# Local attention in blocks of 32 queries with 160 keys, one relative mask, and one DMA round trip for q and k

## The chip, the cores and the metric

The kernel runs on one core of one Trainium2 chip, as one program in fp32. The metric is device time in microseconds (us) of that core, the median of several runs. TensorE (PE in the rows, PEld for its weight loads), VectorE (DVE), ScalarE (ACT) and GpSimd (POOL) compute; SyncE (SP) issues the DMAs of the stage that is changed. The two "streams" below are the two batches.

## The reference, cut to what matters

A first part (a recurrent attention layer) is not touched. The second part has two layers; in each, after the projection of q, k and v (8 heads of 64), q and k are normalised and rotated, and every query sees the keys of its own window of 128 and of the window before, as far as they are at most 128 positions back:

```python
bk, bv = (look_around(bk), look_around(bv))        # the window before, and the own one
sim = jnp.einsum('bhwid,bhwjd->bhwij', bq, bk)     # bq is q * 8
i = bt[:, :, None]
j = btk[:, None, :]
mask = (i < j) | (i > j + WINDOW) | (j == -1)      # WINDOW = 128
sim = jnp.where(mask, -jnp.finfo(sim.dtype).max, sim)
attn = jax.nn.softmax(sim, axis=-1)
out = jnp.einsum('bhwij,bhwjd->bhwid', attn, bv)
```

Then follow the output projection, a layer norm, and a gated MLP (hidden size 682). There are 2 batches of 4096 positions, so 32 windows for each batch and layer.

## The kernel before

The program has five stages: `setup`, `mix`, `scan`, `gate`, and `local`, which holds both layers of the second part and takes the span from about 2257 us to its end. Only `local` is changed.

`local_stage` steps through 64 units (u = 0 to 63: 32 windows of layer 0, then 32 of layer 1) for each of two streams s. A **half-step** `half(s, u, w, l)` does the attention of stream s, unit u (w = u % 2 is the slot of its keys), and beside it the end of the attention and the MLP of the other stream o (unit `um`), and projects stream s's next unit. There are 128 half-steps. Each engine runs its own list of work per half-step, and each list is written out by hand, in a `half` for each engine; semaphores tie them. No engine overtakes in its own list.

TensorE's list is: `values` of o for head pairs 0 and 1; `scores` of s for pairs 0 and 1; (layer 1: `turn_out`); `values` 2 and 3; `scores` 2 and 3; `project_out`; `project` k, `mean`, `project` v, `variance`, `project` q; `hidden`; `out`. `scores(2)` and `scores(3)` wait until `row_max` has emptied the PSUM banks of two pairs before.

q and k come out of VectorE's 32x32 block transposes (`turn_q`, `turn_k`) and need the blocks moved between partition quarters. This is done by a DMA round trip through DRAM: SP writes `q1` to `qz` and reads it back in four DMAs into `qT` (`write_q`, `read_q`), and so with k (`kz`, `kT`, at a later place of the list). The probabilities go the same way: `turn_p` turns one pair of heads into `pb`, `write_p` writes a group g of two pairs, `read_p` reads it back in four DMAs into `pT`; `values` waits for them. SP's list is: `read_q`; a store; loads of the next window; `write_p` 0; `write_k`; `write_p` 1; `read_p` 0; `read_k`; `read_p` 1; `write_q`. A read waits first until the write has landed.

For the scores of one head, 64 rows of `qT` are the weights (64x128) and 256 keys (two slots of 128) stream past them. The two heads of a pair lie in the two row halves of the array. `row_max` adds the mask and takes the maximum, `exponent` (ScalarE) and `normalise` (GpSimd) work on 256 keys a head. Since the slot of a window's own keys alternates, there is a mask for each slot order, and `remask` rewrites a half of one.

## Time and profile before

| | us |
|---|---|
| median of 3 runs | 4971.94 |
| lowest, highest | 4968.18, 4976.64 |
| the profiled execution | 4966.22 |
| span of the profiled execution | 4964.4 |
| `local` stage, from its first GpSimd instruction to the end | 2256.95 to 4964.4 |

The profile page gives busy time by engine over the span; since the five stages differ, the stretches of the local stage are read apart. A timeline lists instructions of one engine in order of time, merged where one follows another of the same kind; an fp32 matmul stands in it as two records, each with its weight load on PEld. In SP's timeline the time is that in which SP is held by issuing, not that of the transfer.

### The profile page before, as it was taken

The numbers are of one execution on the slowest core, as the hardware profiler recorded it, in microseconds if no ns is written. First come the engines' busy times: TensorE is split into PE (matmuls) and PEld (weight loads), VectorE is DVE, ScalarE is ACT, GpSimd is POOL, SyncE is SP. The second block draws the span as 40 slices with busy tenths as digits, with TensorE's granted clock in tenths as the row PEclk, the third lists the DMA queues.
The fourth block names the chain that finished last, engine by engine and source line by source line (L and its number), as shares of the span: only waits on it lengthen the run. The fifth ranks groups of instructions, "written<-read, shape, count | busy, mean of one in ns | idle before, by whom it ended". The sixth has DMA issues, their size and how long they took to land. (4 is left out here: it accounts for less than half of the span.)

```text
span 4964.4 us, 269505 instructions
## 1 busy us (share of the span) xinstructions
PE 4507.8 (91%) x107928; PEld 3817.4 (77%) x107928; DVE 3564.7 (72%) x10345; ACT 2979.7 (60%) x8486; POOL 2441.6 (49%) x3196
## 2 busy tenths in 40 slices
PE   7898898678888888666999999999999999999998
PEld 6888888678888888654777777777777777777777
DVE  4666666568878887475777777777777777777775
ACT  5777777534444444354666666666666666666665
POOL 1222222267777777203555555555555555555554
PEclk8999999789999999788999999999999999999999
DMA  2343343467777777694555666555565555555554
GB/s 87 87 96 93 93 98 89 114 143 165 165 165 163 167 164 161 175 299 126 170 170 168 173 174 171 172 171 171 180 196 175 173 173 172 171 171 173 173 175 131
DMA packets 1283528, 775.96 MB, mean 156 GB/s; under 512 B 686800, under 2 KB 1179088, under 8 KB 1282256
## 3 DMA queue, kind: packets, MB, share of 16 engines
q1 hardware_dynamic: 1231888, 700.43, 53.1%
q10 hardware_dynamic: 51392, 73.02, 5.0%
q14 instruction: 190, 1.56, 0.1%
q8 instruction: 58, 0.95, 0.1%
HBM read 410.44 MB, written 362.68 MB: 156 GB/s over the span
## 5 line engine op out<-in xcount | busy, mean ns | idle before, releaser
L2367 ACT ACTIVATE l_prob<-l_prob,l_nb,l_rq 128x256 f32<-128x256 f32 x1024 | 601.6, 590 | 20.8 <-DVE l_nb L2193 13.1
L2033 POOL TENSOR_TENSOR l_prob<-l_prob,l_rinv 128x512 f32<-128x512 f32 x512 | 526.8, 1039 | 108.4 <-DVE l_rinv L2173 108.4
L2017 POOL TENSOR_TENSOR l_k<-l_kn,l_tab 128x512 f32<-128x512 f32 x128 | 162.5, 1270 | 614.8 <-DVE l_kn L2165 614.8
L2559 PE MATMUL lD<-l_hid,w 128*128 128x128 f32 x3072 | 364.0, 275 | 0.0
L2559 PEld LDWEIGHTS lD<-l_hid,w 128*128 128x128 f32 x3072 | 353.3, 192 | 0.0
L2551 PEld LDWEIGHTS lA<-l_hn,w 128*128 128x128 f32 x2048 | 242.9, 195 | 110.1 <-POOL l_hn L2051 61.1
L2202 DVE STREAM_TRANSPOSE l_pb<-l_prob 128x512 f32<-128x512 f32 x512 | 326.6, 676 | 0.6 <-POOL l_prob L2033 0.5
L2027 POOL TENSOR_TENSOR l_qr<-l_q 128x512 f32<-128x512 f32 x128 | 162.4, 1269 | 328.1 <-DVE l_q L2131 328.1
L1097 POOL TENSOR_TENSOR sc_aqx<-sc_late,sc_headmask 128x256 f32<-128x256 f32 x256 | 170.8, 667 | 278.9 <-PE sc_Y L1190 277.2
L1173 PE MATMUL sc_AB<-sc_aq,sc_bkx 32*32 32x32 f32 x16384 | 257.3, 198 | 37.4 <-POOL sc_bkx L1097 29.1
L497 POOL TENSOR_TENSOR rk<-rk,bkraw 128x256 f32<-128x256 f32 x64 | 54.6, 871 | 477.9 <-DVE bkraw L383 477.9
L2551 PE MATMUL lA<-l_hn,w 128*128 128x128 f32 x2048 | 266.0, 284 | 11.8 <-POOL l_hn L2051 5.2
L1115 POOL TENSOR_TENSOR sc_bkT<-sc_tok,sc_headmask 128x128 f32<-128x128 f32 x512 | 263.2, 534 | 0.0
L2524 PE MATMUL lD<-l_oT,wo 128*128 128x128 f32 x2048 | 262.6, 281 | 0.1
L2524 PEld LDWEIGHTS lD<-l_oT,wo 128*128 128x128 f32 x2048 | 238.2, 191 | 29.2 <-issue 28.9
L2473 PE MATMUL lB<-wqkv,l_h 128*128 128x512 f32 x512 | 242.9, 597 | 17.4 <-DVE l_mask L2262 17.2
L2551 PE MATMUL lB<-l_hn,w 128*128 128x128 f32 x2048 | 250.9, 276 | 0.0
L1173 PEld LDWEIGHTS sc_AB<-sc_aq,sc_bkx 32*32 32x32 f32 x16384 | 213.3, 108 | 39.4 <-issue 38.6
L2473 PE MATMUL lC<-wqkv,l_h 128*128 128x512 f32 x512 | 241.0, 593 | 0.0
L2473 PE MATMUL lA<-wqkv,l_h 128*128 128x512 f32 x512 | 240.9, 593 | 0.0
L2551 PEld LDWEIGHTS lB<-l_hn,w 128*128 128x128 f32 x2048 | 240.5, 193 | 0.0
L2193 DVE TENSOR_TENSOR l_nb<-l_mx,l_nrq 128x2 f32<-128x2 f32 x512 | 220.6, 431 | 17.7
(276 smaller groups left out, 13707.3 us busy)
## 6 DMA issues: line engine op xcount, KB each, us to landing
scratch_pz<-l_pb SPq DMA_DIRECT2D x256, 512.0 KB, 3.0
l_pT<-scratch_pz SPq DMA_DIRECT2D x1024, 128.0 KB, 3.2
scratch_cm<-cm SPq DMA_DIRECT2D x64, 512.0 KB, 4.1
scratch_qz<-l_q SPq DMA_DIRECT2D x128, 256.0 KB, 2.9
l_qT<-scratch_qz SPq DMA_DIRECT2D x512, 64.0 KB, 2.0
scratch_kz<-l_k SPq DMA_DIRECT2D x128, 256.0 KB, 2.8
l_kT<-scratch_kz SPq DMA_DIRECT2D x512, 64.0 KB, 2.9
sc_early<-scratch_cm ACTq DMA_DIRECT2D x59, 512.0 KB, 4.7
```

The lines of the kernel that those rows point to most:

```text
L1097: return nc.gpsimd.tensor_tensor(dst[:], src.unsqueeze(2).broadcast_to([P, 2 * BG, HQ, CH]), headmask[:].unsqueeze(1).unsqueeze(3).broadca ...
L1115: last = nc.gpsimd.tensor_tensor(bkT[c % 2][:, b * BG:(b + 1) * BG], tok[k][:, c, b, 1:3].rearrange("p x g i -> p (x g) i").unsqueeze(2) . ...
L1173: last = mm(AB_ps[c][at, (x * BG + q) * QH:(x * BG + q + 1) * QH], bkx[c][at, 2 * q + x].rearrange("p h t -> p (h t)"), aq[c][at, q], star ...
L2017: tt(k1[s][:], kn[s][:], wide(2, slice(0, DH)), ALU.mult)
L2033: tt(prob[s][:, pair], prob[s][:, pair], rinv[s][:, pair].unsqueeze(2).broadcast_to([P, 2, 2 * P]), ALU.mult).then_inc(Q["pn"][s].sem, 1)
L2193: tt(nb[s][:, pair], mx[s][:, pair], nrq8[s][:, pair], ALU.mult).then_inc(Q["nb"][s].sem, 1)
L2202: nc.vector.transpose(pb[s][:, g, :, at:at + 2].rearrange("p j h x t -> p (h x) j t"), prob[s][:, 2 * hp:2 * hp + 2].rearrange("p h (x j k ...
L2367: last_ = nc.scalar.activation(prob[s][:, h], prob[s][:, h], ACT.Exp, scale=rq8[s][:, h:h + 1], bias=nb[s][:, h:h + 1], accum_out=sums[s][ ...
L2473: last_ = mm(bank[s][j][:], h[:, k * P:(k + 1) * P], wqkv[:, k, j * INNER:(j + 1) * INNER], start=(k == 0), stop=(k == CC - 1))
L2524: last_ = mm(bank[s][3][:, m * P:(m + 1) * P], wo[:, k, m * P:(m + 1) * P], oT[s][:, k], start=(k == 0), stop=(k == NHP - 1))
L2551: last_ = mm(bank[s][j][0:MW, at:at + P], w1[:, k, tile * MW:(tile + 1) * MW], hn[s][:, k], start=(k == 0), stop=(k == CC - 1))
L2559: last_ = mm(bank[s][3][:, c * P:(c + 1) * P], w2[:, m, c * P:(c + 1) * P], hid[s][:, m], start=(c == 0 and m == 0), stop=(c == CC - 1 and ...
```

## The change

- **Scores.** Each block of 32 queries meets only the 160 keys (5 blocks of 32) that it can see. A head pair takes 8 matmuls of 64x32 weights and 160 columns instead of 2 of 64x128 and 256. The block i of queries writes PSUM partitions 32i to 32i + 31, columns 0 to 159.
- **Mask.** The position of a key among the 160 is relative to the block, so one mask serves all windows, with a second one for the first window. The masks per slot order and `remask` go.
- **Keys in three slots.** `qkT` holds three slots of four blocks, q and k side by side. A window with w = 1 lands in slot 1, one with w = 0 in slot 2, and its k also in slot 0, by four more reads.
- **One round trip for q and k.** `turn_q` and `turn_k` write one tile `qk`; `write_qk` (where `write_k` stood) writes it in one DMA, `read_qk` (where `read_k` stood) reads both with rows of 1024 bytes. `turn_q` now writes its blocks in the order that `turn_k` had.
- **Probabilities.** `prob` and `pb` hold 160 keys a head. For each quarter of the partitions the values need two rectangles of `pz`, one for each key slot, so `read_p` issues eight DMAs a group. The rest of `pT` is never written and is zeroed at the start.
- On TensorE each wait ahead of scores is followed by a `sem_inc` of its own.

```diff
+    NR = BL + 1
+    SPAN = 32 * NR
...
-        qT, kT = two("qT", [P, P, NHP]), two("kT", [P, 2, BL, NHP, 32])
-        V, prob = two("V", [P, 2, HEADS, DH]), two("prob", [P, HEADS, 2 * P])
-        pb, pT = two("pb", [P, 2, BL, NHP, 2, 32]), two("pT", [P, 2, BL, NHP, 2, 32])
+        qk, qkT = two("qk", [P, BL, 2, NHP, 32]), two("qkT", [P, 3 * BL, 2, NHP, 32])
+        V, prob = two("V", [P, 2, HEADS, DH]), two("prob", [P, HEADS, SPAN])
+        pb, pT = two("pb", [P, 2, NR, NHP, 32]), two("pT", [P, 2, BL, 2, NHP, 32])
...
+                def read_qk(s, u, w):
...
+                    turned = a["qkz"][s].rearrange("(i c) (j n) -> j c i n", i=BL, j=BL)
+                    cur = (2, 1)[w] * BL
                     for j in range(BL):
...
+                        sp.dma_start(qkT[s][32 * j:32 * j + 32, cur:cur + BL].rearrange("p i y h t -> p i (y h t)"),
+                                     turned[j]).then_inc(S["qkT"][s].sem, 16)
+                    if w == 0:
+                        for j in range(BL):
+                            sp.dma_start(qkT[s][32 * j:32 * j + 32, 0:BL, 1].rearrange("p i h t -> p i (h t)"),
+                                         turned[j][:, :, 32 * NHP:]).then_inc(S["kT"][s].sem, 16)
...
                     for j in range(BL):
-                        sp.dma_start(pT[s][32 * j:32 * j + 32, g].rearrange("p i h x t -> p i (h x t)"),
-                                     a["pz"][s, g].rearrange("(i c) (j n) -> j c i n", i=BL, j=BL)[j]).then_inc(H[g]["pT"][s].sem, 16)
+                        for slot, lo, hi in ((0, 0, j + 1), (1, j, BL)):
+                            start = at + lo * 32 * row + (j + BL * slot - lo) * n
+                            sp.dma_start(pT[s][32 * j:32 * j + 32, g, lo:hi, slot].rearrange("p i h t -> p i (h t)"),
+                                         bass.AP(a["pz"].tensor, start, [[row, 32], [32 * row - n, hi - lo], [1, n]])
+                                         ).then_inc(H[g]["pT"][s].sem, 16)
...
-                        for t in (kT[s], V[s]):
+                        for t in (qkT[s], V[s], pT[s]):
                             nc.gpsimd.memset(t[:], 0.0)
...
-                                                               in1=mask[s][w][:].rearrange("p x n -> p (x n)"), scale=1.0, scalar=3 * MASKED,
+                                                               in1=wm[:, int(u in (0, NW))], scale=1.0, scalar=3 * MASKED,
...
-                    for x in range(2):
-                        rows_ = slice(x * DH, (x + 1) * DH)
-                        last_ = mm(scored(s, hp, x), qT[s][rows_, :, hp], kT[s][rows_, :, :, hp].rearrange("p x i t -> p (x i) t"),
-                                   start=True, stop=True)
+                    own, back = (2, 1)[w] * BL, (1, 0)[w] * BL
+                    for i in range(BL):
+                        for x in range(2):
+                            rows_ = slice(x * DH, (x + 1) * DH)
+                            last_ = mm(scored(s, hp, x)[32 * i:32 * i + 32], qkT[s][rows_, own + i, 0, hp],
+                                       qkT[s][rows_, back + i:back + i + NR, 1, hp], start=True, stop=True)
```

SP's list in a half-step of layer 0, before (`pz` and `l_pT` are the probabilities, `kz` and `l_kT` the keys, `qz` and `l_qT` the queries; 32x4x256 is partitions x blocks x elements of each of the four DMAs):

```order
L1924 DMA scratch_pz<-l_pb 128x1024
L1907 DMA scratch_kz<-l_k 128x512
L1924 DMA scratch_pz<-l_pb 128x1024
L1932 DMA l_pT<-scratch_pz 32x4x256 x4
L1915 DMA l_kT<-scratch_kz 32x4x128 x4
L1932 DMA l_pT<-scratch_pz 32x4x256 x4
L1891 DMA scratch_qz<-l_q 128x512
L1899 DMA l_qT<-scratch_qz 32x4x128 x4
```

The same place after, in a half-step whose partner window has w = 0, from the second write of probabilities to the first read of group 1:

```order
L1921 DMA scratch_pz<-l_pb 128x640
L1933 DMA l_pT<-scratch_pz 32x128
L1933 DMA l_pT<-scratch_pz 32x4x128
L1933 DMA l_pT<-scratch_pz 32x2x128
L1933 DMA l_pT<-scratch_pz 32x3x128 x2
L1933 DMA l_pT<-scratch_pz 32x2x128
L1933 DMA l_pT<-scratch_pz 32x4x128
L1933 DMA l_pT<-scratch_pz 32x128
L1908 DMA l_qkT<-scratch_qkz 32x4x256 x4
L1912 DMA l_qkT<-scratch_qkz 32x4x128 x4
L1933 DMA l_pT<-scratch_pz 32x128
```

Group 0 is eight DMAs instead of four, q and k come in four or eight where k's four stood, and the eight of group 1 follow behind them; the four reads of q at the end of the list have gone.

TensorE around the second pair of `values`, layer 1, before (`lD<-ident` is `turn_out`, `l_pT,l_V` is `values`, `lD<-l_oT` is `project_out`):

```order
L2567 MATMUL lD<-ident,l_hout 128x128 x2
L2516 MATMUL lB<-l_pT,l_V 64x128 x8
L2498 MATMUL lB<-l_kT,l_qT 128x256
L2498 MATMUL lC<-l_kT,l_qT 128x256
L2498 MATMUL lA<-l_kT,l_qT 128x256 x2
L2524 MATMUL lD<-l_oT,wo 128x128 x8
```

The same place after:

```order
L2504 MATMUL lB<-l_pT,l_V 64x128 x8
L2486 MATMUL lB<-l_qkT 32x160
L2486 MATMUL lC<-l_qkT 32x160
L2486 MATMUL lB<-l_qkT 32x160
L2486 MATMUL lC<-l_qkT 32x160
L2486 MATMUL lB<-l_qkT 32x160
L2486 MATMUL lC<-l_qkT 32x160
L2486 MATMUL lB<-l_qkT 32x160
L2486 MATMUL lC<-l_qkT 32x160
L2486 MATMUL lA<-l_qkT 32x160 x8
L2512 MATMUL lD<-l_oT,wo 128x128 x8
```

The four score matmuls of two head pairs have become sixteen small ones; `values` ahead of them and `project_out` behind keep their places.

## Rows read from the trace of the kernel before

**Rows 1.** Section 1 of the page: busy us, share of the span, instructions.

```profile
PE 4507.8 (91%) x107928; PEld 3817.4 (77%) x107928; DVE 3564.7 (72%) x10345; ACT 2979.7 (60%) x8486; POOL 2441.6 (49%) x3196
```

**Rows 2.** Windows of layer 0, layer 1: us; busy (count) PE, PEld, DVE, ACT, POOL; PEclk, DMA share, GB/s.

```profile
2320.00:3560.00 1240.00, 1230.82 (x8979) 959.45 (x8978) 916.88 (x3115) 821.31 (x2238) 674.88 (x755) 1.00 0.59 172
3620.00:4900.00 1280.00, 1273.99 (x9199) 980.77 (x9199) 981.71 (x3218) 835.97 (x2266) 725.32 (x826) 1.00 0.59 175
```

**Rows 3.** `project_out` in layer 0, in layer 1: min/median/max ns, first and last start.

```profile
L2524 PE MATMUL lD<-l_oT,wo x768: 275/275/377, 2519.5 to 3481.7; 128*128 128x128 f32 x192
...
L2524 PE MATMUL lD<-l_oT,wo x768: 275/275/377, 3708.6 to 4692.4; 128*128 128x128 f32 x192
```

**Rows 4.** Timeline of TensorE, one half-step of layer 0: start us, us, instruction.

```profile
3029.95 2.05 PE L2524 MATMUL lD<-l_oT,wo 128*128 128x128 f32 x16
3031.84 1.88 PE L2473 MATMUL lB<-wqkv,l_h 128*128 128x512 f32 x4
3033.56 0.38 PE L2529 MATMUL lD<-l_x1s,l_mean_w 128*128 128x128 f32 x2
...
3045.59 1.09 PE L2516 MATMUL lD<-l_pT,l_V 128*64 128x128 f32 x16
3046.61 0.60 PE L2498 MATMUL lB<-l_kT,l_qT 64*128 64x256 f32 x1
...
3047.85 1.09 PE L2516 MATMUL lB<-l_pT,l_V 128*64 128x128 f32 x16
3048.88 0.60 PE L2498 MATMUL lB<-l_kT,l_qT 64*128 64x256 f32 x1
...
3050.48 0.38 PE L2524 MATMUL lD<-l_oT,wo 128*128 128x128 f32 x1
```

**Rows 5.** Timeline of VectorE, the same half-step; [idle before it <-who ended it].

```profile
3033.98 0.42 DVE L2228 TENSOR_TENSOR l_dev<-l_x,lD 128x256 f32<-128x256 f32 x1 [1.38 <-PE lD L2529]
...
3034.39 1.28 DVE L2202 STREAM_TRANSPOSE l_pb<-l_prob 128x512 f32<-128x512 f32 x2
3035.60 0.67 DVE L2158 STREAM_TRANSPOSE l_k<-l_kr 128x512 f32<-128x512 f32 x1
```

**Rows 6.** Timeline of SP's queue, the same half-step; us is the issuing time.

```profile
3035.84 0.34 SPq L1924 DMA_DIRECT2D scratch_pz<-l_pb  x1
...
3038.73 1.82 SPq L1932 DMA_DIRECT2D l_pT<-scratch_pz  x4
3040.74 1.73 SPq L1915 DMA_DIRECT2D l_kT<-scratch_kz  x4
3042.64 1.74 SPq L1932 DMA_DIRECT2D l_pT<-scratch_pz  x4
3044.71 0.34 SPq L1891 DMA_DIRECT2D scratch_qz<-l_q  x1
```

**Rows 7.** Section 6 of the page, DMA issues: KB each, median us to landing.

```profile
l_pT<-scratch_pz SPq DMA_DIRECT2D x1024, 128.0 KB, 3.2
...
l_qT<-scratch_qz SPq DMA_DIRECT2D x512, 64.0 KB, 2.0
```

**Rows 8.** Window in the scan, TensorE alone: us, busy (count), PEclk, DMA share, GB/s.

```profile
1500.00:1500.50 0.50, 0.50 (x64) 1.00 0.53 45
```

**Rows 9.** Timeline of GpSimd, start of the local stage.

```profile
2256.95 0.95 POOL L2069 MEMSET l_kT<- 128x1024 f32 x1 [225.59 <-POOLq L104]
```

**Rows 10.** Gate stage: timeline of TensorE, then a window as in rows 2.

```profile
2151.12 0.65 PE L1699 MATMUL ga_Y<-ident,ga_yt 128*128 128x128 f32 x4 [2.15 <-DMA ga_yt<-scratch_y_tok]
...
2156.54 0.65 PE L1699 MATMUL ga_Y<-ident,ga_yt 128*128 128x128 f32 x4 [0.92 <-DMA ga_yt<-scratch_y_tok]
...
2161.77 0.86 PE L1699 MATMUL ga_Y<-ident,ga_yt 128*128 128x128 f32 x4 [2.41 <-DMA ga_yt<-scratch_y_tok]
...
2145.00:2175.00 30.00, 20.43 (x90) 16.47 (x90) 21.22 (x59) 17.57 (x48) 0.00 (x0) 0.84 0.98 299
```

More of the change, by code:

```diff
@@ L1761, in local_stage @@
         rot, tab = two("rot", [P, 4, DH]), two("tab", [P, 4, DH])
-        wm = one("wm", [P, 2 * P])
+        wm = one("wm", [P, 2, SPAN])
         mean_w, pause, least = one("mean_w", [P, P]), one("pause", [P, NB]), one("least", [P, 1])
         x1s, dsqs = two("x1s", [P, P]), two("dsqs", [P, P])
-        mask = [two(f"mask{s}_", [P, 2, P]) for s in range(NB)]
         hT = [two(f"h{s}_", [P, CC, P + 1]) for s in range(NB)]
@@ L1789, in local_stage @@
         O = signals(nc, ctx, "oT", 2, "lg", ahead=4)
-        H = [signals(nc, ctx, "p_out:16 pT:64", 2, f"lg{g}_") for g in range(2)]
+        H = [signals(nc, ctx, "p_out:16 pT:128", 2, f"lg{g}_") for g in range(2)]
         I = [signals(nc, ctx, "h_in:8 rot_in:8", 2, f"li{w}_") for w in range(2)]
@@ L2071, in first @@
                         nc.gpsimd.memset(x1[s][1][:], 0.0)
-                        nc.gpsimd.memset(mask[s][0][:], MASKED)
                     nc.gpsimd.memset(zero[:], 0.0)
@@ L2181, in row_max @@
                     dve.wait_ge(Q["p_turned"][s].sem, Q["p_turned"][s].after(n, NHP))
-                    if hp == 0 and w == 0:
-                        dve.wait_ge(S["mask0"][s].sem, S["mask0"][s].after(u, 1))
                     nc.vector.memset(pause[:, s:s + 1], 0.0)
@@ L2259, in first @@
                     dve.wait_ge(sems["set"], 1)
-                    for s in range(NB):
-                        nc.vector.tensor_copy(mask[s][0][:, 0, :], wm[:, P:2 * P])
-                        last = nc.vector.tensor_copy(mask[s][1][:].rearrange("p x n -> p (x n)"), wm[:])
-                    last.then_inc(sems["prep"], 1)
-                    dve.wait_ge(sems["prep"], 1)
                     for s in range(NB):
@@ L2316, in half @@
                         gate(o, um, 2, lm)
-                    remask(s, u, w)
                 def last(s, u, w):
@@ L2587, in half @@
                     if mlp:
-                        values(o, um, 0, layer(um, l))
-                        values(o, um, 1, layer(um, l))
+                        values(o, um, wm_, 0, layer(um, l))
+                        values(o, um, wm_, 1, layer(um, l))
                     scores(s, u, w, 0)
@@ L2594, in half @@
                     if mlp:
-                        values(o, um, 2, layer(um, l))
-                        values(o, um, 3, layer(um, l))
+                        values(o, um, wm_, 2, layer(um, l))
+                        values(o, um, wm_, 3, layer(um, l))
                     scores(s, u, w, 2)
@@ L2624, in last @@
                     for hp in range(NHP):
-                        values(s, u, hp, 1)
+                        values(s, u, w, hp, 1)
                     turn_out(1 - s, u)
@@ L2707, in lay_out @@
     out["eye16"] = np.ascontiguousarray(np.broadcast_to(np.eye(CH, dtype=np.float32), (P, 2, CH, CH)))
-    q, kx = np.arange(P)[:, None], np.arange(P)[None, :]
-    neg = np.float32(MASKED)
-    before, own = np.where(kx < q, neg, 0), np.where(kx > q, neg, 0)
-    out["winmask"] = np.concatenate([before, own], axis=1).astype(np.float32)
+    row, r = np.arange(P)[:, None], np.arange(160)[None, :]
+    neg, behind = np.float32(MASKED), r - row % 32
+    near = np.where((behind < 0) | (behind > P), neg, 0)
+    begin = np.where(r < P - row // 32 * 32, neg, near)
+    out["winmask"] = np.stack([near, begin], axis=1).astype(np.float32)
     n = out["x"].shape[1]
```

99 lines of the change are left out of this document (41 added, 58 removed).

## The prediction, made before the changed kernel was run

> **What bounds the kernel now.** I read the page's busy shares first, then stretches of the local stage, and then one half-step engine by engine. TensorE is busy 91% of the span, and 99% of the local stage at full granted clock, where VectorE has 74 to 77% and the DMA engines 59% [rows 1, 2]. A half-step (one window of one batch) lasts (3481.7 - 1.8 - 2519.5)/47 = 20.43 us in layer 0 and (4692.4 - 1.8 - 3708.6)/47 = 20.89 us in layer 1 [rows 3]; 1.8 us is from the first to the last record of one `project_out`. I count time in a half-step from the start of `project_out`, 3029.95, as T [rows 4]. TensorE goes from group to group with hardly a hole; the next `project_out` is at T+20.53.
>
> One other chain is nearly as long, and the change touches all of it. VectorE turns the first two head pairs at T+4.44 (3034.39), behind `deviate`, which waits for the mean matmul at T+3.61 [rows 4, 5]. SP writes `pb` at T+5.89, and when that has landed it reads group 0 back from T+8.78, then k from T+10.79, then group 1 from T+12.69 [rows 6]. Four reads hold SP 1.73 to 1.82 us, that is 0.47 us from one to the next, whether each carries 64 or 128 KB, while a single 512 KB write holds it 0.34 us [rows 6, 7]. So **a read costs SP a fixed time, whatever its size**. The last read of group 1 begins at about 12.69 + 3 x 0.44 = T+14.0; at the median 3.2 us to landing [rows 7] it is there at T+17.2, and TensorE wants it at T+17.90 (3047.85) [rows 4]. The slack is 0.7 us.
>
> **The change part by part.**
>
> Scores on TensorE. Now the two pairs of heads at T+16.66 take 1.24 us (3046.61 to 3047.85), and the two at T+18.93 take 1.60 us (3048.88 to 3050.48), because the last waits for `row_max` [rows 4]. A record of 512 columns takes 1.72/4 = 0.43 us [rows 4], so one of 160 takes 0.134 us. If the eight 64x32 tiles of a head pair run side by side, two records in each are 0.27 us a pair, against 0.46 now. If the four column tiles ran one after the other, they would be 4 x 2 x 0.134 = 1.07 us. Issue is no limit: in the scan 64 matmuls of 32x32 tiles begin in 0.50 us [rows 8], so 16 records are issued in 0.13 us. The scan also shows column tiles side by side, and so does `values`, with 16 records of 128 columns in 1.03 us [rows 4]; so I take 0.30 us, and 0.9 us for two pairs with the change of tile shape. The Trainium skill, TensorEngine Tiling (Array Packing), Instruction Overhead, puts about 60 cycles on each matmul; by that rule (an estimate from the page) 64 records of a half-step would cost 1.6 us in overhead alone and eat the gain, but the scan's pace is far below it. So TensorE needs 0.3 us less ahead of the second pair of `values`, and some 0.7 us less after it, where the wait for `row_max` goes too.
>
> Softmax. Rows of 160 instead of 256 elements shorten `row_max`, exp, normalise and the turn. `turn_p` takes 0.605 us for 512 elements [rows 5]; for 320 the bounds are 0.378 (all of it per element) and 0.605; I take 0.40. Only the first two turns lie on the chain: -0.4 us, so the write of group 0 goes out at T+5.5. The other savings are on engines that wait anyhow, and `deviate` still holds the turns until T+4.44. `remask`, the two mask copies and `turn_q`'s odd pattern leave VectorE, off the path.
>
> The write of `pb` is 320 KB instead of 512. It took 3038.73 - 3035.84 = 2.89 us from issue to the first read [rows 6]; the floor is 2.0, the median of a quiet 64 KB read [rows 7]. I take 2.5, nearer to the row with the same route: first read at T+8.0.
>
> **Reading p back takes eight DMAs a group instead of four**, since each quarter of partitions needs two rectangles. The bytes fall, the number doubles. At the measured step a group holds SP 0.35 + 7 x 0.47 = 3.6 us instead of 1.8, and this for both groups. q and k come in 4 reads (1.73 us) where k's were; at w = 0 four more fetch the third slot (+1.9 us). q's own write goes, and its reads behind it, but the write stood at T+14.8 [rows 6], after group 1 had been issued, so their going shortens nothing on this chain. In numbers: group 0 from T+8.0 to 11.65; 0.2 for the waits; q and k to 13.6 or 15.5; 0.15; the last read of group 1 begins 0.35 + 6 x 0.47 = 3.2 later, at T+16.9 or 18.9. Landing lies between 2.0 us and 3.2 us [rows 7]; the pieces are small and the engines less loaded, so I take 2.2: group 1 is there at **T+19.1 or T+21.1**. TensorE wants it at T+17.6 in layer 0, T+18.0 in layer 1 (a `turn_out` more).
>
> So the second pair of `values` becomes the place where TensorE waits, and all later work stands behind it in order: values 1.03, scores 0.9, next `project_out`. The period becomes 21.0 or 23.0 us, 22.0 on average, in both layers alike; halves with the third slot (two in four) are the long ones. Group 0 is due at about 8.0 + 3.2 + 2.2 = T+13.4 against T+15.64, and qkT at 13.2 + 2.9 = T+16.1 against T+16.66: both in time, k's narrowly.
>
> Start. `first` clears 3 x 1024 elements of `qkT` for each stream instead of 1024, and 2048 of `pT` besides: 8192 elements more, at 0.95 us per 1024 [rows 9] 7.6 us, and TensorE waits for them; the two mask fills of 256 and the mask copies give back between 0.5 and 2: +6 us.
>
> TensorE's clock. In the gate stage TensorE waits 2.15 us, 0.92 us, 2.41 us, with 2161.77 - 2151.12 = 10.65 us from one long wait to the next, and the granted clock is 0.84 there: after the long waits it stands at its 1.2 GHz level for a while, which costs 0.16 x 10.65 = 1.7 us each time [rows 10]. The new waits are about 1.3 us in short halves and 3.2 in long ones. Bounds: nothing, and 1.7 us for each of 126 half-steps = 214 us. The long waits are nearer to the gate's, the rest of the half-step is denser than there: I take 1.7 us in 48 of the 64 long ones, +80 us.
>
> Sum, against the profiled execution (4966.2 us, span 4964.4): 63 x (22.0 - 20.43) = +99; 63 x (22.0 - 20.89) = +70; +6; +80; together +255, 5221 us. The median of the runs is 6 us above the profiled execution: 5227, and I give 5225.
>
> **The rivals.**
>
> (a) SP's step does not bind, and TensorE's gain shows. This is so if the reads, most of them of fewer pieces than now, cost SP the 0.34 us of a lone issue and land in 2.0. Then the last read begins at T+8.0 + 2.7 + 0.2 + 1.4 + 0.15 + 2.4 = 14.9, landed T+16.9, in time; the long halves at T+18.3 are 0.3 to 0.7 late. TensorE's saving of about 0.7 us a half-step remains in most: 4972 + 6 - 126 x 0.65 = 4895 us. It decides from 14 reads at under 0.37 us each. Against it: the step is the same for 64 and 128 KB, so it does not hang on how much a read moves; the 0.34 us were seen only where no other read followed at once. The Trainium skill, DMA: Bandwidth & Descriptors, Issuing engines are not separate DMA queues, says that the issuing time is usually small beside the DMA, which would give this case; here the trace disagrees, 1.8 us of issuing stand beside 3.2 of landing. Chance 0.10.
>
> (b) The two cancel: a step of about 0.40 and fast landing, period near 20.6: 4972, within 0.2%. Chance 0.04.
>
> (c) The column tiles don't overlap in the 64x32 shape: 1.07 instead of 0.30 us for each of the two pairs after the wait, 126 x 1.54 = +194 on the forecast: 5420. Speaks for it: four streams of 64 rows at once stand nowhere in the trace. Against: the scan and `values`. Chance 0.06.
>
> **How the numbers follow.** The forecast, with or without the clock term, has 0.80. Its own range is 5130 (neither clock loss nor slower landing) to 5380 (clock in every half). Landing at 3.2 adds 1.0 x 126. Slower has 0.80 + 0.06 = 0.86, same (within 0.2%, what a measurement of this kernel can tell from no change) 0.04, faster 0.10. Below 5060 lie (a), (b) and a little of the forecast, above 5410 (c): the range is 5060 to 5410.
>
> **What would show it.** Right: SP's row of group reads x8 with 3.6 us each; `values` waiting for DMA `l_pT` by 1 to 4 us in nearly each half-step; periods of two lengths, 2 us apart, alike in both layers; scores of two head pairs in about 0.9 us. The clock term: granted clock below 1.00 in the local stage. Wrong: SP issuing eight reads in under 2.8 us, or TensorE without idle time ahead of the second pair of `values`.

## The result and the profile after

| | before | after |
| --- | --- | --- |
| median of the runs, us | 4970.42 (4968.18 to 4976.64) | 5243.18 (5233.22 to 5257.45) |
| span of the profiled execution, us | 4964.4 | 5255.7 |
| half-step in layer 0 / layer 1, us | 20.43 / 20.89 | 22.64 / 22.65 |
| granted clock in the local stage | 1.00 | 0.95 / 0.94 |

The changed kernel is slower: ratio 1.0549, 95% interval 1.0522 to 1.0576. It takes 273 us more; 5225 was predicted, in the range 5060 to 5410. The half-step's means were taken from all starts of `project_out` in the middle of each layer (2420 to 3520 and 3950 to 5150 in the changed kernel). Its layer 1 begins near 3776 us, so the first 150 us of the second window below still belong to layer 0. The lines of the changed kernel shift: values are L2504, scores L2486, `project_out` L2512, the reads of p L1933, those of q and k L1908, of the third slot L1912.

Two windows of the changed kernel, layer 0 and layer 1, with the columns of [rows 2]:

```profile
2320.00:3560.00 1240.00, 1093.68 (x10687) 833.55 (x10668) 709.18 (x2790) 703.70 (x2020) 539.05 (x683) 0.95 0.41 124
3620.00:4900.00 1280.00, 1135.78 (x10985) 863.36 (x10981) 764.37 (x2883) 714.63 (x2053) 582.73 (x742) 0.94 0.42 131
```

TensorE was busy 99% of layer 0 in [rows 2], and is busy 1093.68/1240 = 88% now; every engine has less to do in the same stretch, the DMA engines too (0.41 for 0.59). So neither a computing engine nor the DMA engines are overloaded: something is waited for. SP's queue and TensorE over one long half-step and the start of the next, to set beside [rows 4, 6]; T counts from 3031.23:

```profile
3038.12 0.35 SPq L1921 DMA_DIRECT2D scratch_pz<-l_pb  x1
...
3040.56 3.72 SPq L1933 DMA_DIRECT2D l_pT<-scratch_pz  x8
3044.46 1.74 SPq L1908 DMA_DIRECT2D l_qkT<-scratch_qkz  x4
3046.24 1.85 SPq L1912 DMA_DIRECT2D l_qkT<-scratch_qkz  x4
3048.28 3.62 SPq L1933 DMA_DIRECT2D l_pT<-scratch_pz  x8
```

```profile
3031.23 3.37 PE L2512 MATMUL lD<-l_oT,wo 128*128 128x128 f32 x16
...
3048.13 1.09 PE L2504 MATMUL lD<-l_pT,l_V 128*64 128x128 f32 x16
...
3053.21 1.09 PE L2504 MATMUL lB<-l_pT,l_V 128*64 128x128 f32 x16 [2.54 <-DMA l_pT<-scratch_pz]
...
3055.29 3.30 PE L2512 MATMUL lD<-l_oT,wo 128*128 128x128 f32 x16
```

Eight reads hold SP 3.6 to 3.7 us where four held it 1.8 (over the whole stage the median is 3.8 for group 0 and 3.6 for group 1). From 3040.56 to 3051.90 it does hardly anything but issue: twenty-four reads, one after the other. Group 1's last one begins at about T+20.2, and TensorE has stood idle for 2.54 us when the values of pair 2 start at T+21.98; before, they started at T+17.90 [rows 4]. The wait adds up, in the list of TensorE's waits (total us, times, longest):

```profile
PE lB L2504 <- DMA l_pT<-scratch_pz: 244.7, 125, 4.1
```

In the kernel before the same line read:

```profile
PE lB L2516 <- DMA l_pT<-scratch_pz: 8.7, 15, 1.3
```

And `project_out`, 2.05 us in [rows 4], takes 3.30 to 3.37 us behind the wait, though it is the same work: the granted clock, 1.00 up to the wait's end, is 0.83 and then 0.58 on average, so mostly at the lower of its two levels (1.2 and 2.4 GHz). The columns are those of [rows 2]:

```profile
3053.20:3055.20 2.00, 1.99 (x48) 1.42 (x48) 0.31 (x4) 0.85 (x4) 0.29 (x1) 0.83 0.55 131
3055.30:3058.40 3.10, 3.10 (x21) 3.10 (x17) 1.27 (x10) 3.10 (x13) 0.72 (x1) 0.58 0.02 5
```

The means over each kind of half-step of layer 0, from the same trace (us; T from each half-step's own start):

| | period | last group 1 read begins | group 1 there | values of pair 2 | lost to the clock |
| --- | --- | --- | --- | --- | --- |
| before, layer 0 | 20.4 | 14.2 | 17.4 | 17.9 | 0.00 |
| short, after a short one | 20.8 | 17.2 | 19.0 | 19.0 | 0.03 |
| short, after a long one | 21.5 | 17.9 | 19.7 | 19.7 | 0.66 |
| long | 24.2 to 24.4 | 19.3 to 19.9 | 21.1 to 21.6 | 21.1 to 21.7 | 1.9 |

"Lost to the clock" is the sum over the half-step of (1 - granted clock) x time. The two kinds alternate in pairs, as the program has the third slot's reads in two half-steps of four.

### The profile page after: what moved, and what is told of

Same layout as the page of the kernel before. It is cut to its first block and busy times, and to the rows that moved or that the text cites. A ratio compares the mean times of both kernels' runs of the same rounds, so it can differ in the third digit from the quotient of the medians.

```text
span 5255.7 us, 282935 instructions
## 1 busy us (share of the span) xinstructions
PE 4476.4 (85%) x114072; PEld 3759.9 (72%) x114072; DVE 3289.0 (63%) x10277; ACT 2888.6 (55%) x8486; POOL 2286.1 (43%) x3196
## 5 line engine op out<-in xcount | busy, mean ns | idle before, releaser
L2344 ACT ACTIVATE l_prob<-l_prob,l_nb,l_rq 128x160 f32<-128x160 f32 x1024 | 518.2, 510 | 14.3 <-DVE l_nb L2185 14.3
L2027 POOL TENSOR_TENSOR l_prob<-l_prob,l_rinv 128x320 f32<-128x320 f32 x512 | 362.8, 719 | 340.0 <-DVE l_rinv L2167 339.9
L2504 PE MATMUL lB<-l_pT,l_V 128*64 128x128 f32 x2048 | 184.9, 338 | 244.7 <-DMA l_pT<-scratch_pz 244.7
L2353 ACT COPY l_oT<-lB 128x256 f32<-128x256 f32 x128 | 47.6, 372 | 591.8 <-PE lB L2504 591.8
L2504 PEld LDWEIGHTS lB<-l_pT,l_V 128*64 128x64 f32 x2048 | 145.1, 170 | 280.7 <-DMA l_pT<-scratch_pz 280.4
L2178 DVE CUSTOM_DVE_ANT_0 l_prob<-lB,l_wm 128x160 f32<-128x160 f32 x256 | 81.7, 319 | 414.6 <-issue 398.8
L2512 PEld LDWEIGHTS lD<-l_oT,wo 128*128 128x128 f32 x2048 | 286.1, 224 | 48.3 <-issue 31.4
L2512 PE MATMUL lD<-l_oT,wo 128*128 128x128 f32 x2048 | 310.5, 313 | 0.1
L2450 PE MATMUL lB<-wqkv,l_h 128*128 128x512 f32 x512 | 244.2, 600 | 23.0 <-POOL l_mean_w L2068 21.3
```

The costliest lines, as they stand in the source:

```text
L2027: tt(prob[s][:, pair], prob[s][:, pair], rinv[s][:, pair].unsqueeze(2).broadcast_to([P, 2, SPAN]), ALU.mult).then_inc(Q["pn"][s].sem, 1)
L2344: last_ = nc.scalar.activation(prob[s][:, h], prob[s][:, h], ACT.Exp, scale=rq8[s][:, h:h + 1], bias=nb[s][:, h:h + 1], accum_out=sums[s][ ...
L2450: last_ = mm(bank[s][j][:], h[:, k * P:(k + 1) * P], wqkv[:, k, j * INNER:(j + 1) * INNER], start=(k == 0), stop=(k == CC - 1))
L2504: last_ = mm(valued(s, hp)[x * DH:(x + 1) * DH], V[s][:, (1 - w, w)[slot], 2 * hp + x], pT[s][:, g, :, slot, at + x], start=(slot == 0), s ...
L2512: last_ = mm(bank[s][3][:, m * P:(m + 1) * P], wo[:, k, m * P:(m + 1) * P], oT[s][:, k], start=(k == 0), stop=(k == NHP - 1))
```

## Experiments

**The order of SP's reads.** The third slot's reads (`read_third`, four DMAs, needed only one half-step later) stand behind group 1's.

```diff
                     if within(un):
                         read_qk(o, un, wn)
                     read_p(s, u, 1)
+                    if within(un):
+                        read_third(o, un, wn)
```

> The changed kernel with one thing moved: the four reads of the third key slot stand behind group 1's reads on SP instead of in front of them. Bytes, packets, instructions and semaphores are the same. Theory A (SP's fixed time of about 0.45 us for each read in front of group 1's last one sets the half-step): the long half-steps lose 4 x 0.46 = 1.9 us of wait and, with the shorter wait, most of the low clock behind it (1.7 us), and become like the short ones, 20.8 and 21.5 us instead of 24.2: 64 x 3.1 = about 200 us less, 5045 us; group 1 is in SBUF at T+19 in every half-step. If only the order counts and the clock stays as it is: 64 x 1.9 = 120 less, 5120. Theory B (the small tiles of the scores cost TensorE the time) and theory C (the bytes and packets of all reads together are the limit): no change, 5240 us.

Measured: 5028.61 us, ratio 1.0114 (1.0086 to 1.0142), 215 us less than the changed kernel. Layer 0 and layer 1:

```profile
2320.00:3400.00 1080.00, 987.80 (x10080) 753.23 (x10065) 663.91 (x2618) 659.92 (x1891) 508.01 (x641) 0.99 0.44 134
3600.00:4700.00 1100.00, 1020.60 (x10300) 774.46 (x10299) 723.59 (x2708) 674.01 (x1931) 551.60 (x704) 0.99 0.46 144
```

The granted clock is back at 0.99, the two lengths of half-step are gone (means of 20.9 to 21.3 us for the four kinds, 21.1 in all), and group 1 is there at T+19.1 to 19.3. The same bytes through the same engines in another order: this cannot be the tiles, and not the amount of data. It fits theory A to 16 us.

**The number of reads, in the kernel before.** Nothing of the change is in it; each read of p is cut in two.

```diff
-                        sp.dma_start(pT[s][32 * j:32 * j + 32, g].rearrange("p i h x t -> p i (h x t)"),
-                                     a["pz"][s, g].rearrange("(i c) (j n) -> j c i n", i=BL, j=BL)[j])
+                        for i in (slice(0, 2), slice(2, 4)):
+                            sp.dma_start(pT[s][32 * j:32 * j + 32, g, i].rearrange("p i h x t -> p i (h x t)"),
+                                         a["pz"][s, g].rearrange("(i c) (j n) -> j c i n", i=BL, j=BL)[j][:, i])
```

> The kernel before with each read of p cut into two of half the size: 8 reads a group instead of 4, the same bytes in the same packets, the same scores, TensorE's work untouched. Theory A: four issues more in front of group 0's end and eight in front of group 1's, 8 x 0.47 = 3.8 us; group 1 would be there at T+21.1 instead of T+17.3, which is where the changed kernel's long half-steps have it, so the half-step becomes about 24 us with the clock's share (between 23 without it and 25.5): 126 x 3.4 = +430 us, about 5400 us (5250 to 5550). Theory B (TensorE's small tiles) and theory C (bytes and packets): within 20 us of 4970.

Measured: 5303.08 us, ratio 1.0669 (1.0651 to 1.0687). SP's queue, then TensorE in the same half-step:

```profile
3010.20 3.66 SPq L1933 DMA_DIRECT2D l_pT<-scratch_pz  x8
3014.05 1.73 SPq L1915 DMA_DIRECT2D l_kT<-scratch_kz  x4
3015.96 3.77 SPq L1933 DMA_DIRECT2D l_pT<-scratch_pz  x8
```

```profile
3021.33 1.09 PE L2517 MATMUL lB<-l_pT,l_V 128*64 128x128 f32 x16 [2.05 <-DMA l_pT<-scratch_pz]
...
3024.07 3.14 PE L2525 MATMUL lD<-l_oT,wo 128*128 128x128 f32 x16
```

Doubling the reads alone makes the old kernel slower by more than the whole change does, in the same way: 3.7 us of issuing, a wait of 2 us at the values of pair 2, a slow `project_out` behind it. The size was 97 us under the expectation: the half-steps of layer 0 are 23.2 us rather than 24, since the smaller pieces land 2.0 us after their issue where the old ones took 3.2 [rows 7], so group 1 is there at T+20.3 and not at T+21.1.

**The bytes, with the number of reads kept.** Each read of the changed kernel brings 16 of its 32 rows; the other rows keep old contents, so that half of p's way back is left out.

```diff
-                            sp.dma_start(pT[s][32 * j:32 * j + 32, g, lo:hi, slot].rearrange("p i h t -> p i (h t)"),
-                                         bass.AP(a["pz"].tensor, start, [[row, 32], [32 * row - n, hi - lo], [1, n]])
+                            sp.dma_start(pT[s][32 * j:32 * j + 16, g, lo:hi, slot].rearrange("p i h t -> p i (h t)"),
+                                         bass.AP(a["pz"].tensor, start, [[row, 16], [32 * row - n, hi - lo], [1, n]])
```

> The changed kernel with each of the eight reads of p a group bringing only 16 of its 32 rows: as many issues, half of the packets and bytes (the values then use old contents for the other rows; that part of the result is left out). Theory A (issues): the last read is still issued at T+17.2 and T+19.2, the landing behind it is up to 0.5 us shorter: 0 to 60 us less than the changed kernel, 5180 to 5240. Theory C (packets and bytes of the reads): group 1 is there 1.5 to 2.5 us earlier, 190 to 300 us less and the clock's share on top: 4900 to 5050.

Measured: 5224.18 us, ratio 1.0497 (1.0471 to 1.0522). Half of the data is worth 19 us, eight reads hold SP as long as before (3.6 to 3.8 us), and the wait is still there:

```profile
PE lB L2504 <- DMA l_pT<-scratch_pz: 229.3, 125, 4.1
```

Theory C, the bytes and packets, is out for this kernel.

**Fewer but larger reads.** p stands in DRAM with zero blocks beside it, so four reads of 128 KB bring a group, with 1024-byte pieces; two writes of 256 KB put it there. The third slot's reads are behind.

```diff
-                    sp.dma_start(a["pz"][s, g], pb[s][:, g].rearrange("p r h t -> p (r h t)"))
+                    z = a["pz"][s, g].rearrange("p (d y n) -> p d y n", d=7, y=2)
+                    for y in range(2):
+                        sp.dma_start(z[:, 3 - 3 * y:7 - 3 * y, y], pb[s][:, g, y:y + BL].rearrange("p r h t -> p r (h t)"))
...
                     for j in range(BL):
-                        for slot, lo, hi in ((0, 0, j + 1), (1, j, BL)):
...
+                        sp.dma_start(pT[s][32 * j:32 * j + 32, g].rearrange("p i y h t -> p i (y h t)"),
+                                     bass.AP(a["pz"].tensor, at + (3 + j) * n, [[row, 32], [32 * row - n, BL], [1, n]])
```

> The changed kernel with both suspected costs taken away: p lies in DRAM with zero blocks beside it (written once at the start), so that a key block's band is one read with 1024-byte packets, 4 reads a group instead of 8, for one write more per group (two of 256 KB instead of one of 320 KB); and the third slot's reads stand behind group 1's. Theory A: group 1's last read is issued 8 x 0.46 = 3.7 us earlier for the reads, 2 x 0.47 later for the writes, 1.9 earlier for the order, so group 1 is there at about T+17 instead of T+21 and T+19; nothing waits then but as in the kernel before (T+17.8 is when values of pair 2 are wanted), and the half-step is bounded by TensorE: 20.4 us or less, down to 19.8 if the shorter scores come through (two pairs in front of the values take 1.06 us here). 4830 to 4970 us, likeliest 4900, with the granted clock at 1.00. Theory B (TensorE's small tiles cost the time): 5200 or more. Theory C (bytes): the reads move 256 KB a group more in zero blocks, so no gain over the changed kernel, 5240 or more.

Measured: 5181.65 us, ratio 1.0424 (1.0407 to 1.0441). This is 153 us slower than the version with eight reads and the same order, so the expectation missed, and by a lot. The reads were indeed issued early, the last at T+15.7, but they landed at T+20.0. The DMA issues of the changed kernel, then of this one (KB each, median us to landing; of the changed kernel's 2048 reads of p the page shows the 512 largest, the others carry 16, 32 and 48 KB):

```profile
scratch_pz<-l_pb SPq DMA_DIRECT2D x256, 320.0 KB, 2.9
...
l_qkT<-scratch_qkz SPq DMA_DIRECT2D x512, 128.0 KB, 2.8
...
l_pT<-scratch_pz SPq DMA_DIRECT2D x512, 64.0 KB, 2.0
```

```profile
scratch_pz<-l_pb SPq DMA_DIRECT2D x512, 256.0 KB, 3.5
l_pT<-scratch_pz SPq DMA_DIRECT2D x1024, 128.0 KB, 3.7
...
l_qkT<-scratch_qkz SPq DMA_DIRECT2D x512, 128.0 KB, 3.6
```

Group 0 could be read from T+9.5 only, not T+8.0, and every transfer took 0.6 to 1.7 us longer, those of q and k too, which were not touched (128 KB of p took 3.2 us in the kernel before [rows 7], 3.7 here). The DMA engines' share of the layer is 0.64 here:

```profile
2320.00:3550.00 1230.00, 1097.66 (x10748) 834.24 (x10748) 729.87 (x2798) 709.54 (x2034) 540.69 (x684) 0.96 0.64 161
```

TensorE waits twice in a half-step, longest for q and k, and then still for group 1:

```profile
PE lB L2500 <- DMA l_qkT<-scratch_qkz: 214.8, 127, 16.6
PE lB L2518 <- DMA l_pT<-scratch_pz: 74.2, 113, 2.0
```

So both limits exist, and lie close together: with eight small reads SP is late, with twice the bytes the transfers are. The time of an issue is not quite fixed either: group 0's four reads, behind two writes, hold SP 2.5 us here (median), group 1's four the usual 1.73. How much of it is the cut-up write and how much the reads' zero blocks was not separated.

**TensorE's clock, first try.** Ten fp32 matmuls whose result nobody reads stand in front of the values of pair 2, to keep TensorE busy in the wait.

```diff
                     if mlp:
+                        fill(o, um, 20)
                         values(o, um, wm_, 2, layer(um, l))
...
+                        for _ in range(n // 2):
+                            mm(bank[s][1][:, 0:P], mean_w[:], mean_w[:], start=True, stop=True)
```

> The changed kernel with ten fp32 matmuls of 128x128 by 128 on TensorE, into columns of a bank that nothing reads any more, in front of the values of pair 2, where TensorE waits for group 1. They are about 2.2 us of TensorE work that computes nothing of the result and lie in the wait of the long half-steps (3 us); in the short ones (wait about 1 us) up to 1 us of them can stick out. If TensorE's clock falls because of the wait: granted clock 1.00 in the local stage instead of 0.94, values of pair 2 1.09 us instead of 1.98 and project_out 2.05 instead of 3.37, long half-steps 22.5 instead of 24.2, 64 x 1.7 = 110 us less, given back in part by up to 64 x 1 us in the short ones: 5130 to 5200 us. If the clock does not hang on the wait: no gain, 5240 to 5310 us with the clock at 0.94.

Measured: 5411.03 us, ratio 1.0881 (1.086 to 1.0901), slower than either theory has it. Two things went wrong. The filling took 2.5 us at the full clock, so that it stuck out of the short half-steps by 2 us. And the program became longer by 80 matmuls: of the page's two kinds of instruction transfers, the changed kernel's and then this one's,

```profile
q8 instruction: 71, 1.16, 0.1%
```

```profile
q8 instruction: 291, 4.77, 0.4%
```

with, in this kernel, a wait of TensorE that the changed kernel does not have, and that stands in one of the four half-steps of the loop:

```profile
PE lD L2504 <- issue: 81.4, 24, 3.9
```

It waited 3.4 us each time (81.4/24) for nothing that the profile shows, and lost its clock there; that it had run out of instructions is inferred from the two together. As a test of the clock this run is inconclusive, though most of the other half-steps had a granted clock of 1.00.

**The clock, second try.** Two matmuls of 512 columns instead (2.0 us), in two of four half-steps.

```diff
                     if mlp:
+                        if wm_ == 1:
+                            fill(o, um, 2)
...
+                            mm(bank[s][1][:], mean_w[:], wqkv[:, 0, 0:INNER], start=True, stop=True)
```

> The changed kernel with two fp32 matmuls of 128x128 by 512 on TensorE in front of the values of pair 2, in the long half-steps alone: 2 x 1.19 = 2.4 us of work that computes nothing of the result, inside a wait of about 3 us, with few instructions (the first try had 80 more matmuls in the loop's four half-steps, this has four). If TensorE's clock falls because of the wait: granted clock 1.00 or nearly, long half-steps 22.5 instead of 24.2, short ones behind them 0.7 less: 64 x (1.7 + 0.4) = 130 us less than the changed kernel, 5110 (5080 to 5160), and group 1 still waited for at T+21. If the clock is no cost of its own (the DMA chain sets the time in any case): 5240, same as the changed kernel. If the first try was slow because filling itself delays something and not for its instruction fetches: 5350 or more.

Measured: 5257.15 us, ratio 1.0566 (1.0548 to 1.0584). The condition was mistaken: it hits one long half-step and one short one. But that gives a comparison inside one run. In layer 0 the filled long half-step takes 23.03 us with 0.18 lost to the clock, the long one beside it without filling 24.05 with 1.70 lost (in the changed kernel both take 24.2 to 24.4), and group 1 is there at T+21.1 and T+21.0, equally late.

**The clock, third try.** The condition is `if wm_ == o`, which is true in the two long half-steps.

> The changed kernel with two fp32 matmuls of 128x128 by 512 (2.4 us, nothing of the result) in front of the values of pair 2 in the half-steps in which group 1 waits behind the third slot's reads; the try before had them in one of the two long half-steps and in one short one. Clock as a cost of its own: in the first layer both long half-steps 23.0 us instead of 24.2 and the short ones unchanged at 20.7 and 21.0, mean 21.9 instead of 22.65, granted clock near 1.00; in the second layer the same less what instruction fetches of the longer program cost: 5240 - 63 x 0.75 x 2 + 60 = 5145 to 5210 us. Clock not a cost of its own: mean half-step of the first layer 22.65, 5240 to 5300 us.

Measured: 5178.99 us, ratio 1.0415 (1.0398 to 1.0433): 64 us faster than the changed kernel, by adding work. Layer 0:

```profile
2320.00:3550.00 1230.00, 1131.32 (x11104) 841.12 (x11104) 732.47 (x2858) 723.07 (x2073) 554.58 (x701) 0.99 0.43 129
```

```profile
3024.63 1.98 PE L2513 MATMUL lB<-wqkv,l_mean_w 128*128 128x512 f32 x4
3027.69 1.09 PE L2504 MATMUL lB<-l_pT,l_V 128*64 128x128 f32 x16 [1.07 <-DMA l_pT<-scratch_pz]
...
3029.41 2.05 PE L2519 MATMUL lD<-l_oT,wo 128*128 128x128 f32 x16
```

`project_out` is back at 2.05 us. The long half-steps take 22.9 and 22.8 us instead of 24.2 and 24.4, the mean is 21.86 (21.9 expected). In layer 1 the mean is 22.52, for 22.65 in the changed kernel, so little is gained there. Four stops of up to 4.6 us in front of the values of pair 0, of the kind of the first try, are part of it; that they are instruction fetches (107 of the transfers shown above) is again inferred.

**Issuing from a second queue.** In the version with the third slot behind, three of group 1's eight reads go out from ACT's queue.

```diff
                     if mlp:
                         gelu(o, um, 0, layer(um, l))
+                    act.wait_ge(H[1]["p_out"][s].sem, H[1]["p_out"][s].after(u))
+                    act.wait_ge(Q["pv"][s].sem, Q["pv"][s].after(u * NHP + 3, NHP))
+                    read_part(act, s, 1, (0, 1))
                     if mlp:
                         gelu(o, um, 1, layer(um, l))
+                    read_part(act, s, 1, (2,))
```

> The changed kernel with the third slot's reads behind group 1's, and three of group 1's eight reads issued by ACT's queue (two behind its first gelu, where ACT stands idle for 1.1 us, one behind its second), five by SP. Bytes and number of reads are unchanged. Theory A (SP's 0.47 us for each issue, and not the transfers, sets when group 1 is there): 3 x 0.47 = 1.4 us off SP, its last read issued at T+15.9 instead of T+17.3 and landed at about T+17.9 instead of T+19.2; the half-step goes from 21.1 to about 19.8 (values of pair 2 at T+18.1, the rest of the half-step 1.72 as in the undisturbed ones), 126 x 1.3 = 165 us less than the 5029 of that version: about 4865, with the clock at 1.00; faster than the kernel before by some 2%. Rival: the issues hold ACT as long as SP, its gelus come later and TensorE's last block of the hidden layer and the residual with them: 4950 to 5050. Rival (transfers are the limit): 5030, landing still at T+19.

Measured: 4923.67 us, ratio 0.9897 (0.988 to 0.9913). It beats the kernel before, by 1.0%, but not by the 2% expected: 20.06 us in layer 0, 20.53 in layer 1. Group 1 is no longer what TensorE waits for; now it is idle in front of the scores of pair 0. They start at T+17.25 in layer 0, 0.7 us behind the time at which TensorE is ready.

```profile
PE lB L2503 <- DMA l_qkT<-scratch_qkz: 71.1, 52, 16.6
...
PE lB L2503 <- issue: 35.5, 72, 2.1
```

The landing of q and k is only the start of this wait. They are there at T+16.54 on average, ahead of TensorE's T+16.55 in 40 of 57 half-steps. Behind their wait TensorE's list has three or four further waits, each with the `sem_inc` that the change put there, and the queue passes them at 0.15 us each: in the half-step from 2988.70, q and k land at T+16.30, the queue's records follow at T+16.33, 16.49, 16.64, 16.79 and 16.94, and the scores start at T+17.04. From landing to scores it is 0.6 us in half the cases and 0.75 in the others, in the changed kernel as here; in the kernel before, which has no such `sem_inc`, it was 0.09 where k landed last (T+16.84 to T+16.93 in the half-step from 4816.23). So some 0.5 us of the wait belong to the change's last point and not to the DMAs. Putting the wait for q and k last in the list, or leaving those `sem_inc` out, was not tried.

**q and k sooner.** SP issues them between the first and the last four of group 0's reads.

```diff
                         read_qk(o, un, wn)
+                    read_part(sp, s, 0, range(4, 8))
                     read_p(s, u, 1)
```

> The version with three of group 1's reads on ACT's queue, with one thing moved: SP issues the four reads of q and k between the first four and the last four of group 0's reads, instead of behind all eight. Theory A (what is late now is whatever SP issues last in front of its use): q and k are there at about T+14.5 instead of T+16.7, group 0 at about T+15.0 (wanted at T+15.5), so the scores of pair 0 start at T+16.5 instead of T+17.3, values of pair 2 at T+17.8 to 18.0 instead of T+18.1 to 18.5; group 1 (there at T+17.9) is again the last, and the half-step loses 0.1 to 0.5 us: 4924 - 126 x 0.3 = about 4885 us (4860 to 4915). Rival: group 0 lands after T+15.5 and TensorE waits there instead: 4930 to 5000.

Measured: 4924.32 us, ratio 0.9898 (0.9882 to 0.9915), no change, and 9 us beyond the upper end expected. The rival came true in its mechanism: the wait moved.

```profile
PE lD L2522 <- DMA l_pT<-scratch_pz: 92.0, 125, 6.7
```

TensorE now waits 0.7 us for group 0 (values of pair 0 at T+16.2 instead of T+15.5) and none for q and k. Whatever of SP's first twelve reads is last is late: the order among them gives nothing.

**Four and five reads on ACT's queue.** ACT issues two of group 0's reads in front of its first gelu and two of group 1's behind it; with five, a third of group 1's follows behind the second gelu.

```diff
+                    act.wait_ge(H[0]["p_out"][s].sem, H[0]["p_out"][s].after(u))
+                    act.wait_ge(Q["pv"][s].sem, Q["pv"][s].after(u * NHP + 1, NHP))
+                    read_part(act, s, 0, (0, 1))
                     if mlp:
                         gelu(o, um, 0, layer(um, l))
```

> As the version with three reads on ACT's queue, but ACT issues two of group 0's reads (in front of its first gelu) and two of group 1's (behind it), SP six and six. Theory A: SP is through with group 0 and reaches q and k 0.9 us earlier (T+11.2 instead of T+12.1), so they are there at about T+15.8 and the scores of pair 0 no longer wait (T+16.5 instead of T+17.2); group 1's last read is again issued at about T+15.9 and landed at T+17.9, values of pair 2 at T+18.0 instead of T+18.1 to 18.5: 4924 - 126 x 0.2 = about 4900 (4870 to 4920). Rival: ACT's first gelu, 0.9 us later, makes the hidden layer's last block and group 0's values late: 4925 to 4980.

> As the one before it, with a third read of group 1 on ACT behind the second gelu, SP six and five: group 1's last read issued at T+15.4 and landed at T+17.4, the last wait is gone, values of pair 2 at T+17.5 to 17.7, and the half-step is TensorE's own, about 19.5 us: 4924 - 126 x 0.6 = about 4850 (4820 to 4890). Rival: the third gelu, 0.5 us later, makes the residual and the next values late by as much: 4890 to 4950.

Measured: 4838.7 us, ratio 0.974 (0.9727 to 0.9753), with four, and 4842.86 us, ratio 0.9747 (0.9733 to 0.976), with five. The version with four is the fastest of all and 2.6% faster than the kernel before. Its layer 0, layer 1, queues and TensorE:

```profile
2320.00:3400.00 1080.00, 1068.12 (x10871) 809.51 (x10870) 733.18 (x2829) 720.11 (x2058) 549.87 (x696) 1.00 0.48 146
3500.00:4500.00 1000.00, 986.34 (x9971) 742.50 (x9972) 702.68 (x2622) 651.71 (x1871) 534.94 (x682) 1.00 0.49 152
```

```profile
3024.52 1.17 ACTq L1857 DMA_DIRECT2D l_pT<-scratch_pz  x2
3024.57 3.02 SPq L1857 DMA_DIRECT2D l_pT<-scratch_pz  x6
...
3027.47 0.80 ACTq L1857 DMA_DIRECT2D l_pT<-scratch_pz  x2
...
3027.94 1.73 SPq L1919 DMA_DIRECT2D l_qkT<-scratch_qkz  x4
...
3029.84 2.66 SPq L1857 DMA_DIRECT2D l_pT<-scratch_pz  x6
```

```profile
3032.15 1.09 PE L2523 MATMUL lD<-l_pT,l_V 128*64 128x128 f32 x16
...
3033.95 0.51 PE L2505 MATMUL lA<-l_qkT 64*32 64x160 f32 x16
3034.39 1.09 PE L2523 MATMUL lB<-l_pT,l_V 128*64 128x128 f32 x16
...
3036.60 2.05 PE L2531 MATMUL lD<-l_oT,wo 128*128 128x128 f32 x16
```

TensorE is busy 99% again at a granted clock of 1.00, no wait for p of any weight is left, and a half-step takes 19.39 us in layer 0 and 19.82 in layer 1, about 1.06 less than before in both: 126 x 1.06 = 134 us, and 4970 - 134 = 4836. This is the gain of the shorter scores that the late reads had covered; how much of it is the small tiles and how much the shorter wait for `row_max` was not separated. The step from three to four gave 85 us where 24 were expected: a wait of 0.7 us went in nearly each half-step (126 x 0.7 = 88), which the expectation had written down as a start at T+16.5 instead of T+17.2 and then not put into the sum. q and k are there at T+15.7, early enough for the queue to be through its list of waits when TensorE is ready. The fifth read brought nothing, since nothing waited any more.

## Why the prediction was right, step by step

- **A read costs SP 0.47 us, whatever its size.** Held: x8 rows of 3.6 to 3.8 us against 3.6, and the same 0.47 us behind reads of 32, 48 and 64 KB (the first step of each row, behind a read of 16 KB, is 0.38). The one exception on record is group 0 of the version with zero blocks, four reads in 2.5 us. It is the step on which the rest rests, and three runs show it as the cause and not as a companion: more issues with equal bytes (+330 us in the kernel before), fewer bytes with equal issues (-19 us), the same issues spread over two queues (the whole wait gone). The Trainium skill, DMA: Bandwidth & Descriptors, Issuing engines are not separate DMA queues, says that issuing from several engines saves only the sequencer's time to initiate, usually small beside the DMA. The first half agrees with what was seen, since that time is what was saved; the second does not hold here: from the version with the third slot behind to the one with four reads on ACT's queue it is 190 us of 5029.
- **Turns, write and group 0.** Two turns take 0.88 us where they took 1.28 [rows 5]: -0.40, as predicted. First read at T+7.8 to 8.0 where the clock is full (predicted 8.0), group 0 there at T+13.1 to 13.9 (13.4): held, and never waited for.
- **Group 1.** Last read at T+17.2 and, in the long ones, T+19.3 to 19.9 (16.9 and 18.9), there at T+19.0 and 21.1 to 21.6 (19.1 and 21.1): held, though the long ones' last read is 0.4 us late behind a short half-step and 1.0 behind a long one, whose slow clock still delays the next start. Landing took 1.8 us and not 2.2, which made good the 0.3 us by which SP was later.
- **Two lengths of half-step, alike in both layers.** Held: 20.8 and 21.5 against 24.2 to 24.4, mean 22.64 and 22.65. Without the clock's part the sum had 22.0; the kernel with the waits filled shows 21.86 in layer 0.
- **The clock.** The term was 80 us. The filled kernel gains 22.64 - 21.86 = 0.78 us a half-step in layer 0, which would be 98 us over 126. Over the whole kernel it gained 64, as it gained little in layer 1. The form of the term was right too: 1.9 us are lost in the long half-steps, 0.7 in the short ones behind them, hardly any elsewhere. That the long waits cause it is shown by the filled kernels.
- **The sum, and some luck.** With its clock term the forecast had a mean half-step of 22.0 + 80/126 = 22.63 us; 22.64 and 22.65 were measured. So close a fit is luck in part: by the filled kernel the clock's share was some 18 us larger, and the rest (21.86 for 22.0) as much smaller. The 18 us between forecast and result lie outside the middle of the layers: fourteen half-steps around the change of layer, from 3577 to 3921 us, take 24.5 us on average in the profiled execution (20.8 for the fourteen around it in the kernel before), some 26 us more than the same number elsewhere. Why they are slow was not examined. The profiled execution is also 14 us above the median.
- **The scores.** Two head pairs take 0.86 us from their start to the values of pair 2 in the version with four reads on ACT's queue (layer 0), and 0.89 to `project_out` (0.9 predicted), against 1.31 and 1.56 before. The predicted saving of 0.3 and 0.7 us a half-step was 0.45 and 0.67. The reading that 64 small matmuls begin in 0.50 us in the scan was too high, as [rows 8] count all that are under way in the window; 46 begin in it. That changes nothing in the sum. Rival (c), column tiles one after the other, is out. The estimate from the Trainium skill, TensorEngine Tiling (Array Packing), Instruction Overhead, 1.6 us of overhead in a half-step, does not fit: both blocks together take 1.75 us with all of their work, which would leave 0.15 us for it if it came on top.
- **q and k "in time, narrowly".** This one failed. They were there at T+16.4 to 17.1 (16.1 predicted, wanted at T+16.66), and the scores of pair 0 started at T+17.1 to 18.0. It cost nothing only because group 1 was later still; it was the next wait in line as soon as group 1's was gone, and it held back the version with three reads on ACT's queue. The landing term was right (3.0 us for 2.9); SP's last issue of them began at T+13.4 to 14.1 instead of 13.2. And the prediction let the scores start at the landing, and put the waits with their `sem_inc` at nothing; the runs show 0.6 to 0.75 us between the two.
- **The start.** TensorE's first wait of the stage grew from 17.2 to 21.3 us, 4 us where 6 were predicted; the next one, for q and k, grew from 14.9 to 16.7, and counted from the end of the stage before, the first `project_out` comes 10 us later.
- **Rivals (a) and (b)** would have needed 14 reads at under 0.37 us, or a step of 0.40. The step was 0.47.

## What to carry to other kernels

Count DMA issues per loop pass before counting bytes: on one queue each costs about 0.47 us of the issuing engine here, so a layout that moves fewer bytes in more pieces can lose more than it saves, and reads that nobody needs soon belong behind those that somebody waits for. When issues are the limit, a second queue with idle time takes them away at hardly any cost; making the pieces larger instead can run into the transfers. When a wait moves, the next one in line is often only a few tenths of a microsecond behind: list all due times of the chain, and not only that of the one that is late. And the time at which data has landed is not yet the time at which work starts: what stands in the engine's list behind the last wait comes in between.

## What the runs showed of the hardware

- **A wait costs more than its length.** The waits of 2.5 us and more in the changed kernel are followed by `project_out` in 3.37 instead of 2.05 us; TensorE's work that nobody needs, 2.0 us in the wait, made the kernel 64 us faster. Waits of about 1 us (the version with the third slot behind) left the granted clock at 0.99.
- **More instructions in TensorE's loop came with stops.** 80 more matmuls in four half-steps brought the page's instruction transfers on q8 from 71 to 291 and stops of up to 3.9 us once in a pass of the loop; with four more there were 107 to 116, and four or five such stops, in layer 1 alone. That the stops are instruction fetches is inferred from the two together.
- **The time to landing was longer where more was under way.** Reads of q and k, unchanged at 128 KB, took 2.8 us at a DMA share of 0.41 and 3.6 us at 0.64.
- **Passing a further wait costs TensorE's queue 0.15 us** in these kernels, where a `sem_inc` follows each: 0.6 to 0.75 us from the landing of q and k to the scores, against 0.09 without them.
- **ACT's queue issues two reads in 0.80 us,** as SP does, when it issues alone, and in 1.05 to 1.17 us while SP issues group 0 beside it; its gelus came late by nothing that TensorE noticed: the half-step of the version with four reads is TensorE's own.
